# Eight input loads moved from the end of a transformer block to its middle, into a buffer that is free by then

## The reference

```
xn = layernorm(x)                                  # x: 8 x 2048 x 1024, f32
att = softmax(einsum('blhd,bmhd->blmh', q, k) * scale, axis=2)
opt = einsum('blmh,blhd->blhd', att, v)            # the sum over m goes over att alone
attn = opt @ w_out.T + b_out
top 2 of 8 experts by xn @ router_w.T, weights by softmax over the two
h1 = gelu(xn @ w1[e].T + b1[e])                    # 1024 -> 4096
y[e] = h1 @ w2[e].T + b2[e]                        # 4096 -> 1024
out = x + attn + sum over e of weight[e] * y[e]
```

## Time and profile before

| what | us |
|---|---|
| median of 2 runs | 4023.27 |
| lowest, highest | 4019.59, 4026.95 |
| the profiled execution | 4020.56 |
| its span, from first to last instruction, core 5 | 4019.0 |
| spans of the eight cores | 4003.7 to 4019.0 |
| TensorE busy | 3773.2 (94%) |
| VectorE, ScalarE, GpSimd busy | 357.0, 606.9, 668.4 |

### The profile page before, as it was taken

How to read it: one execution, slowest core, us unless ns; L and a number is a source line. 1 busy time by engine, 2 the same in 40 slices (tenths; PEclk the granted TensorE clock), 3 DMA queues, 4 the chain that set the end, 5 groups by cost and what they waited for, 6 DMA issues and landing times.

```text
span 4019.0 us, 41883 instructions; the slowest of 8 cores (4003.7 to 4019.0 us)
## 1 busy us (share of the span) xinstructions
PE 3773.2 (94%) x17200; PEld 1685.0 (42%) x17200; DVE 357.0 (9%) x626; ACT 606.9 (15%) x569; POOL 668.4 (17%) x1073
## 2 busy tenths in 40 slices
PE   3788999999999999999999999999999999999994
PEld 2333444444444444444444344444444444444442
DVE  5421100000010000000010100100000010100001
ACT  0230030201102030211202012020201112030200
POOL 1111111111111111111121111212111111111110
PEclk8898999999999999999999999999999999999997
DMA  6553454545454554545457354545545454454544
GB/s 111 81 71 45 71 82 66 87 61 87 66 82 66 76 82 60 87 66 82 66 83 148 42 86 64 82 65 76 84 59 87 66 82 66 71 81 67 86 61 107
DMA packets 255705, 307.07 MB, mean 76 GB/s; under 512 B 51687, under 2 KB 182759, under 8 KB 255520
## 3 DMA queue, kind: packets, MB, share of 16 engines
q0 software_dynamic: 248608, 279.23, 48.0%
q1 hardware_dynamic: 6912, 25.17, 1.9%
HBM read 574.89 MB, written 8.39 MB: 145 GB/s over the span
## 4 chain that ended last, share of the span: by engine, by line
PE 90%; DVE 5%; DMA 2%; issue 1%; ACT 1%; DVEq 0%; SPq 0%; POOL 0%; ACTq 0%; POOLq 0%
PE P L344 43%; PE P L437 43%; DVE scr L451 3%; PE P L377 1%; PE P L188 1%; DMA wvw<-wvf 1%; DMA x_rot<-x 1%; ACT vg L355 1%; DVE scr L535 0%; DVE scr L532 0%; DMA wvw<-w1r 0%; DMA scr<-x 0%; PE P L229 0%; DVE x_rot L484 0%; PE P L383 0%
## 5 line engine op out<-in xcount | busy, mean ns | idle before, releaser
L437 PE MATMUL P<-wvw,vg 128*128 128x512 bf16 x8192 | 1818.6, 383 | 66.8 <-DVE scr L451 51.1
L344 PE MATMUL P<-xnF,wvw 128*128 128x512 bf16 x8192 | 1781.0, 380 | 17.9 <-ACT optF L197 7.1
L437 PEld LDWEIGHTS P<-wvw,vg 128*128 128x128 bf16 x8192 | 804.0, 99 | 1079.1 <-issue 150.3
L344 PEld LDWEIGHTS P<-xnF,wvw 128*128 128x128 bf16 x8192 | 801.2, 98 | 993.2 <-issue 38.1
L355 ACT ACTIVATE vg<-P,b1c_sb 128x1024 bf16<-128x1024 f32 x512 | 570.5, 1114 | 3055.3 <-PE P L344 3054.8
L407 POOL DMA_DIRECT2D wvw<-w2r x512 | 360.1, 706 | 1638.3 <-PE P L437 1566.3
L327 POOL DMA_DIRECT2D wvw<-w1r x512 | 272.1, 534 | 1464.0 <-PE P L344 1459.0
L451 DVE SCALAR_TENSOR_TENSOR scr<-P,wmap_sb,scr 128x512 f32<-128x512 f32 x256 | 192.1, 750 | 3254.2 <-PE P L437 3230.1
L188 PE MATMUL P<-xnF,wvw 128*128 128x512 bf16 x256 | 80.4, 472 | 35.4 <-DMA wvw<-wvf 19.9
L229 PE MATMUL P<-scr 128*128 128x128 f32 x128 | 23.5, 344 | 61.6 <-DVE scr L220 61.6
L188 PEld LDWEIGHTS P<-xnF,wvw 128*128 128x128 bf16 x256 | 27.6, 114 | 80.2 <-issue 65.5
(11 more groups left out here) (41 smaller groups left out, 106.1 us busy)
## 6 DMA issues: line engine op xcount, KB each, us to landing
wvw<-w1r POOLq DMA_DIRECT2D x512, 256.0 KB, 4.3
wvw<-w2r POOLq DMA_DIRECT2D x512, 256.0 KB, 4.3
scr<-x SPq DMA_DIRECT2D x16, 512.0 KB, 4.7
wvw<-wvf POOLq DMA_DIRECT2D x32, 256.0 KB, 5.2
x_rot<-x SPq DMA_DIRECT2D x16, 512.0 KB, 5.4
out<-x_rot SPq DMA_DIRECT2D x16, 512.0 KB, 3.2
wo_sb<-wo POOLq DMA_DIRECT2D x8, 256.0 KB, 14.0
b1c_sb<-b1c POOLq DMA_DIRECT2D x1, 128.0 KB, 15.1
```

The costliest lines, as they stand in the source:

```text
L344: pair=pair: t.matmul(pair[:, j * 512:(j + 1) * 512], w1sl[:, sl * 1024 + fc * 128: sl * 1024 + fc * 128 + 128], xnF[:, fc * T + half * 10 ...
L437: t.matmul(W2B[tl], vg[:, f1c * 1024 + tl * 128: f1c * 1024 + (tl + 1) * 128], w2sl[:, sl * 1024 + (f1c % 2) * 512: sl * 1024 + (f1c % 2) ...
```

## The change

In half 1 the final stage no longer loads x tile by tile into x_rot. The eight tiles of x are loaded by eight DMAs on SP right after emit_outproj(1) is emitted, once TensorE has finished all that was emitted up to there, into xf32, a view of optF as f32 (8192 columns, exactly 8 tiles of 1024). All eight count up one new semaphore, dxf. In emit_final(1) VectorE waits for that count once, adds mixed to x in place in xf32, and SP stores from there. Half 0 stays as it is. The debug dump of optF moves ahead of the loads; it isn't built in the timed kernel.

```diff
-            "dwo", "do0", "do1", "ddbg", "dxp", "dxq")
+            "dwo", "do0", "do1", "ddbg", "dxp", "dxq", "dxf")
...
+    xf32 = optF.bitcast(F32)
+
     def emit_final(half):
         for tl in range(8):
             tt = half * 8 + tl
             par = tt % 2
+            if half == 1:
+                p.wait("vector", "dxf", 16 * 8)
+                xb = xf32[:, tl * 1024:(tl + 1) * 1024]
+                for hh in range(2):
+                    p.wait("vector", "dve", tok_mix[((half, E - 1, hh), tl)])
+                tok_fadd[tt] = p.do("vector", lambda v, xb=xb, tl=tl:
+                                    v.tensor_add(
+                    xb, mixed[:, tl * 1024:(tl + 1) * 1024], xb), inc="dve")
+                p.wait("sync", "dve", tok_fadd[tt])
+                nst[par] += 1
+                p.do("sync", lambda sy, tt=tt, xb=xb: sy.dma_start(
+                    d_out[tt * 128:(tt + 1) * 128, :], xb),
+                    inc=DO[par], inc_by=16)
+                continue
...
         emit_outproj(half)
+        if half == 1:
...
+            p.wait("sync", "pe", p.cnt["pe"])
+            for tl in range(8):
+                p.do("sync", lambda sy, tl=tl: sy.dma_start(
+                    xf32[:, tl * 1024:(tl + 1) * 1024],
+                    d_x[(8 + tl) * 128:(9 + tl) * 128, :]),
+                    inc="dxf", inc_by=16)
         emit_w2(half, 0)
```

More of the change, by code:

```diff
@@ L591, in build_nc @@
         emit_outproj(half)
+        if half == 1:
+            if dbg and DO_B:
+                p.wait("gpsimd", "pe", p.cnt["pe"])
+                tok_dbgo = p.do("gpsimd", lambda g: g.dma_start(
+                    d_dbg_optF, optF), inc="ddbg", inc_by=16)
+                p.wait("sync", "ddbg", tok_dbgo)
+            p.wait("sync", "pe", p.cnt["pe"])
[4 more added lines that the diff above has]
+                    inc="dxf", inc_by=16)
         emit_w2(half, 0)
@@ L602, in build_nc @@
         dumps = [(d_dbg_wmap, wmap_sb), (d_dbg_xnF, xnF)]
-        if DO_B:
-            dumps.append((d_dbg_optF, optF))
         for dst, s_ in dumps:
```

## The result

The changed kernel takes 0.9911 of the time of the kernel before (95% interval 0.9897 to 0.9926). On the median of 4023.27 us that is 3987.5 us: 36 us less, where the forecast was 3990.

A forecast was written before the change was run, and what follows sets the result against it. TensorE's matmul stream was taken to bound the kernel, so only the tail could gain. 4020.56 - 36.06 + 1.0 + 2.2 = 3987.7 us, in terms of the median 3990.4, rounded to 3990 us; range 3982 to 4000.

The forecast's parts named there:

- first rival: At the moved x loads: fair turns between queues, w2 lands in about 5.9 us, no TensorE stall; sum 3988.2 us; chance 0.30.
- the main term: Half 1's tail: last add and its store's issue come 36.06 us earlier, at 3978.71 instead of 4014.77 for the add.
- The two small terms: Costs added to the sum: 1.0 us for final stores in the tail, 2.2 us for TensorE stalling at the moved loads.
- What bounds the tail: Half 1's tail: load, add and store in sequence through two x_rot buffers and SP's queue, 6.48 us a step.
- The adds: Half 1's tail: eight adds of 1.23 us plus 0.10 us between them, 1.33 us a step.
- The stores: Half 1's tail: eight final stores closer together cost from nothing to 2.1 us; 1.0 us taken.
- The lower bound: Final stores in the tail: no added cost if each needs 1.31 us of engine time, under the 1.33 us between issues.
- third rival: Tail: stores can't overlap, 3.2 us each; 22.7 us gained instead of 35.1, time 4002.8 us; chance 0.08.
- The loads: End of half 1's output projection: eight x loads delay w2 landing to 11.8 us, so TensorE stalls 2.2 us.
- the factor 0.85: At the moved loads: 5.2/6.1 from half 0's final; of 9.0 us of x, 7.7 us delay a w2 load.
- The bound of 9.6 us of free time: Weight stream with four slots: a load may take 14.1 - 4.5 = 9.6 us to land before TensorE stalls.
- The other side: Fourth rival, slower than before: x burst starves weights in 2249 to 2270, needing about 35 us of TensorE standing; chance 0.02.

## Why the prediction was right

The forecast was 3990 us and the ratio gives 3987.5, with an interval of 3982 to 3994. So the ratio can't tell the forecast from its first rival; what follows is read from the traces. It was not luck: the main term, 36.06 us, was measured as 36.07. The two small terms were both too dear.

**What bounds the tail: right in the chain, too much laid on the buffers.** Load, add and store one behind the other were the whole of it, and breaking that chain, with the loads still in the tail, took 28.2 us away. The prediction named two causes for it, two x_rot buffers and the order in SP's queue. The rows show the order at work: the slot of the last load was free some 3.5 us before the load was issued, and SP never waited for a slot. The prediction is also wrong in that two x loads were early: by the timeline before, one load was issued behind half 0's last store (at 2162.74) and seven were in the tail. The sum isn't touched by either, since it went from the first add to the last store.

**The adds: right.** 1.33 us a step was forecast and 1.33 was measured. From the first add to the last store's issue are 10.6 us (3977.72 + 9.23 - 0.33 - 3976.02) instead of 46.67, 36.07 less; the working gave 36.06.

**The stores: 1.0 us taken, 0.25 measured.** The last store lands 3989.8 - 3986.62 = 3.18 us after its issue, before it was 2.93. The lower bound, 1.31 us of engine time from the last 2.9 us, was the right one; the 1.59 us of the page's queue row mix in loads. The third rival (a store can't overlap the one before it) is excluded by the 12.1 us for eight.

**The loads: wrong in size, 2.2 us taken, 0 measured on seven cores and 0.8 on one.** The step that failed is the factor 0.85, the share of the x traffic that "came on top" of a weight load's landing, taken from half 0. There x met four extra w2 loads in the weights' own queue, and each needs the other to be felt: the same x traffic beside w1 alone pushed no load past 8.2 us, and eight loads beside the burst gave 5.1 us of wait. At the place of the change w2 landed in at most 9.3 us on core 2 where 11.8 was forecast, 5.2 us late for 9.0 us of x. And more than 9.0 us of x were left by then: the working let the engines run for all of the 4.8 us ahead of the first w2 load, while in 2251 to 2256 their share was 0.60, 3.0 us of work. Of 13.8 us some 10.8 met the weights, so the factor was about 5.2 / 10.8 = 0.5. The bound of 9.6 us of free time was right (9.7 measured). The sum without the 2.2 us, the first rival's, is 3988.2 us; the measured ratio gives 3987.5.

**The first rival: right in its result, half right in its mechanism.** It had the w2 loads land in about 5.9 us; they needed 9.3. The Trainium skill (DMA: Bandwidth & Descriptors, section Queues, rings and completion order) has each DMA engine take turns between queue rows by packet. In the case of twenty loads x drained in 40.5 us, where turns by my packet times gave 50 and x first 29.8. So the rows fit taking turns at a better rate for x than my packet times gave; what sets that rate no run here shows. Nor is it shown that what the profile counts as a packet is the unit in which turns are taken; it counts 6912 / 48 = 144 for a transfer of 128 rows.

**The other side: excluded.** At the moved loads TensorE waited for weights for nothing on core 2 and for 0.8 us on core 0, far from the 35 us that it would take.

## What to carry to other kernels

When the end of a kernel is a chain of load, add and store, ask which wait holds each load back: a slot that isn't free, or only its place behind a store in one engine's stream. Here it was the place, and depth and order together gave four fifths of the gain; a large buffer that has had its last reader gives both. What then remains in the tail is engine time of the DMAs, so loads belong out of it; but place them by the weight bursts, not only by the mean DMA share, since eight loads cost 0 to 0.8 us beside a steady stream and cost 5 us beside a burst of four. And an add to a running sum, as that of x to mixed, can often be done in an idle stretch long before, which was worth another 11.8 us of tail.

## What the runs showed of the hardware

A transfer behind a backlog on one queue lands late, though the engine time in all stays the sum of the parts: a 512 KB store landed in 2.8 to 3.3 us among stores and in 9.2 to 10.0 us when loads were pending ahead of it, at a DMA share of 1.02. And a store's issue took 0.33 us with 1.33 us between issues, but 1.24 us in the median when eight were issued back to back; eight loads back to back took 0.49 in the median. What makes the difference no run shows:

```profile
L624 SPq DMA_DIRECT2D out<-optF x8: 344/1241/1254, 3986.0 to 3992.9; - x8
...
DMA to landing us min/median/max: 3.0/4.9/5.0
```
